# Router logits split into two halves around the last pair of the next batch's input projection (decoder layer, Trainium2)

## The reference

```
x = layernorm(x + mamba(x))          # rmsnorm, in_proj to xi and z (1024 each), causal conv of 4 taps, silu,
                                     # x_proj, softplus(dt), scan over 16 states, y*silu(z), out_proj
x = layernorm(x + depool(x, ctx))    # rmsnorm @ W_in + a decayed sum over context patches + residual
x = layernorm(x + moe(x))            # router: softmax(x @ Wr), 8 experts, top 1, rank in the expert by a
                                     # running count over all tokens, capacity 448, relu MLP 512 -> 2048 -> 512
```

## Time and profile before

| | us |
|---|---|
| median of three runs | 2603.05 |
| the profiled execution, its own time | 2615.71 |
| its span, first to last instruction | 2613.9 |
| PE busy in the span | 2438.4 (93%) |
| DVE busy | 2081.8 (80%) |
| POOL busy | 1786.7 (68%) |
| ACT busy | 1749.5 (67%) |

### The profile page before, as it was taken

The page is one execution under the profiler, slowest core; times in us unless marked ns, Lnnn a source line. Parts: engine busy times, 40 slices in busy tenths (PEclk is TensorE's granted clock), DMA queues, the critical chain, the costliest instruction groups (busy, mean ns, idle before and its releaser), DMA issues.

```text
span 2613.9 us, 33259 instructions
## 1 busy us (share of the span) xinstructions
PE 2438.4 (93%) x11291; PEld 2070.1 (79%) x11291; DVE 2081.8 (80%) x2288; ACT 1749.5 (67%) x4011; POOL 1786.7 (68%) x1045
## 2 busy tenths in 40 slices
PE   7698999999999999999999999997879999999997
PEld 6686787878788787878878787785658989989896
DVE  4899999999999999999999999998833445444452
ACT  5677888888888888888888888887633333333331
POOL 1989999999999999999999999999600101001100
PEclk9899999999999999999999999998979999999998
DMA  6041202212020221202122020211233333234320
GB/s 205 15 132 67 85 15 85 71 36 89 13 91 15 85 75 33 89 18 85 33 75 79 22 92 15 78 50 50 85 127 120 125 125 125 100 128 139 132 75 18
DMA packets 90901, 202.62 MB, mean 78 GB/s; under 512 B 7997, under 2 KB 16843, under 8 KB 90751
## 3 DMA queue, kind: packets, MB, share of 16 engines
q1 hardware_dynamic: 81534, 179.21, 21.1%
q0 software_dynamic: 5120, 14.21, 1.7%
q10 hardware_dynamic: 4096, 7.34, 0.9%
HBM read 171.32 MB, written 29.95 MB: 77 GB/s over the span
## 4 chain that ended last, share of the span: by engine, by line
PE 54%; POOL 25%; DVE 8%; issue 5%; ACT 4%; DMA 3%; SPq 0%; POOLq 0%; DVEq 0%; ACTq 0%
POOL arena L1003 14%; PE work L1683 12%; PE y L1664 11%; PE ring L1683 11%; PE work L1442 7%; PE work L1471 5%; DVE ring L1313 4%; POOL arena L1008 4%; POOL arena L1014 3%; DMA arena<-bc_rows 2%; PE work L1486 2%; ACT ring L858 1%; POOL arena L936 1%; POOL arena L934 1%; POOL arena L932 1%
## 5 line engine op out<-in xcount | busy, mean ns | idle before, releaser
L1003 POOL TENSOR_TENSOR arena<-arena 128x896 f32<-128x896 f32 x512 | 1056.7, 2090 | 20.6 <-PE y L1664 10.1
L858 ACT ACTIVATE ring<-arena,small 128x224 f32<-128x224 f32 x2048 | 794.4, 436 | 138.3 <-DVE arena L1322 106.1
L1313 DVE TENSOR_TENSOR_SCAN ring<-ring,arena 128x896 f32<-128x896 f32 x400 | 809.4, 2024 | 59.3 <-POOL arena L1003 33.5
L1664 PE MATMUL y<-arena,cst_sb 128*128 128x224 f32 x3584 | 775.5, 369 | 75.7 <-POOL arena L1014 57.8
L1664 PEld LDWEIGHTS y<-arena,cst_sb 128*128 128x128 f32 x3584 | 699.5, 199 | 147.4 <-POOL arena L1014 64.1
L1027 POOL DMA_INDIRECT out<-res,ids x32 | 48.9, 1529 | 639.4 <-DVE mst L1368 540.2
L1322 DVE TENSOR_TENSOR arena<-ring,arena 128x896 f32<-128x896 f32 x400 | 433.3, 1083 | 6.0
L1442 PE MATMUL work<-arena 128*128 128x224 f32 x2000 | 428.1, 372 | 6.7 <-DVE arena L1093 6.2
L1442 PEld LDWEIGHTS work<-arena 128*128 128x128 f32 x2000 | 400.9, 203 | 19.1 <-issue 6.8
L1383 DVE SCALAR_TENSOR_TENSOR hidden_lo<-work,hidden_hi 128x448 fp32r<-128x448 f32 x128 | 79.9, 625 | 349.7 <-ACT hidden_hi L902 349.7
L902 ACT ACTIVATE hidden_hi<-work 128x448 fp32r<-128x448 f32 x128 | 69.8, 546 | 374.0 <-PE work L1683 374.0
(11 more groups left out here) (211 smaller groups left out, 3300.3 us busy)
## 6 DMA issues: line engine op xcount, KB each, us to landing
weights<-in_w SPq DMA_DIRECT2D x64, 1024.0 KB, 7.3
arena<-bc_rows SPq DMA_DIRECT2D x128, 448.0 KB, 4.4
arena<-in_ctx SPq DMA_DIRECT2D x16, 896.0 KB, 5.6
expert_rows<-x2e SPq DMA_DIRECT2D x1, 7224.0 KB, 30.1
arena<-in_xT SPq DMA_DIRECT2D x16, 448.0 KB, 6.5
arena<-in_x SPq DMA_DIRECT2D x16, 448.0 KB, 3.7
out<-arena ACTq DMA_DIRECT2D x32, 224.0 KB, 2.3
xrow<-expert_rows SPq DMA_DIRECT2D x7, 903.0 KB, 11.8
```

What stands on the lines that cost most here:

```text
L858: last = nc.scalar.activation(decays[s % 2][:, i * L:(i + 1) * L], delta[:, k, :], ACT.Exp, scale=a_neg[:, n:n + 1])
L1003: nc.gpsimd.tensor_tensor(u[:, u_of(b, s)], dx[:, k:k + 1, :].to_broadcast([P, QN, L]), bc[:, 0, q * QN:(q + 1) * QN, :], ALU.mult).then_i ...
L1313: nc.vector.tensor_tensor_scan(states, h, u_flat[:, u_of(b, s), :], 0.0, ALU.mult, ALU.add).then_inc(scan_done, 1)
L1664: last = nc.tensor.matmul(o, ident, u[:, u_of(b, s), i, :], start=False, stop=(q == Q - 1 and i == QN - 1), skip_group_check=True)
```

## The change

`PE_AT` puts `xi3.0` ahead of the logits, the first half of the logits (`rt.0`) between `xi3.0` and `xi3.1`, and the second half (`rt`) behind `xi3.1`. `routing` on PE gains the place `rt.0` in the steps that have `xi3`; the last batch's step and the drain keep what they had. `FIRST_PART`, which sorts the pieces of a bank, now looks for a part `.0` first; the order in every bank stays as it was.

```diff
         PE_AT = {"xi0.0": 0, "xi0.1": 0.01, "xi1.0": 0.02, "xi1.1": 1, "xi2.0": 1.01, "xi2.1": 1.02, "tx0": 4, "tx1": 4.01,
-                 "rt": 4.02, "xi3.0": 4.03, "xi3.1": 4.04, "out0.0": 6, "out0.1": 7, "out0.2": 7.01, "out0.3": 7.02,
+                 "xi3.0": 4.02, "rt.0": 4.03, "xi3.1": 4.04, "rt": 4.05, "out0.0": 6, "out0.1": 7, "out0.2": 7.01, "out0.3": 7.02,
...
-        FIRST_PART = lambda at, job: at[job if job in at else job + ".0"]
+        FIRST_PART = lambda at, job: at[job + ".0" if job + ".0" in at else job]
...
-                    if b == NB:
+                    if b != LAST and b != NB + 1:
                         yield "rt.0"
                         logits(b, (0,))
                     yield "rt"
-                    logits(b, (1,) if b >= NB else (0, 1))
+                    logits(b, (0, 1) if b == LAST else (1,))
```

## The result

The changed kernel takes 2635.17 us (median of 4 runs, 2626.92 to 2645.29), the kernel before 2603.59 (4 runs). The ratio is 1.0134, 95% interval 1.0111 to 1.0157: slower by 31.6 us, where +14 was forecast (2617 us, range 2594 to 2628). The profiled execution took 2645.29 us with a span of 2643.5, so 29.6 us more than the profiled one before. Both profiled executions are slower than the medians, by 10 and 12 us, so their difference may be read as that of the medians, to some 2 us.

What follows compares the result with a forecast made beforehand. PE, DVE and POOL bound a step in turn. Thirteen steps go from 1477.1 to 11 x 115.11 + 2 x 112.58 = 1491.4 us, +14.3 on the median 2603.05: about 2617 us, range 2594 to 2628.

Steps and rivals of the forecast that it cites:

- the two kinds of steps: Steps before: PE pauses for POOL 28 us after y (mean 112.58 us), or arrives there without a pause (114.37 us).
- The pause of 0.63 us: PE's wait for ACT's copy ahead of the logits; goes, worth 8.2 us at most, taken at nothing.
- The stretch worked out from rows of before: PE from xi3.0 to y, step at 995: done 0.85 us earlier, pause for POOL grows from 1.94 to 2.8 us.
- The falls during xi3 go: Clock falls at the logits or xi3, 9 of 13 steps before, go; they were cheap.
- a fall on y comes in most steps: 3.6 us of quiet ahead of y lowers the clock there; 11 of 13 steps taken.
- The price of such a step: Length of a step whose clock falls on y: 115.11 us, 2.53 us more than one with PE early.
- 312 and 1107: The two steps before whose clock fell on y itself: 115.14 and 115.08 us; 11 steps expected like them.
- The fall behind dt1: Clock fall after the 2.16 us pause ahead of dt1; before, in 7 of 7 late steps, 2 of 5 others.
- the late steps: Steps where PE reaches the next wait for POOL without a pause; seven before, mean 114.37 us.
- that rival: Clock holds ahead of y and every step has PE early: -13.6 us, 2589 us; chance 0.22.
- the second rival: Falls on y replace falls in xi3, as many late steps as before: 2603 us, give or take 3; chance 0.12.
- The third rival: DVE (L1164) waits for the later logits, with the clock as before: +3.9 us, 2607 us; chance 0.06.

Runs made afterwards that it cites:

- mid: Changed kernel with both halves of the logits between xi3.0 and xi3.1; 2607.52 us, ratio 1.0020 to the kernel before.
- fillb3: Changed kernel with the four matmuls of xi3.1 made three times more behind the last logits; 2622.80 us, ratio 1.0083 to the kernel before.
- bdup: Kernel before with the second half of the logits made again behind xi3, their semaphore raised only then; 2628.77 us, ratio 1.0101.
- fillb: Changed kernel with the four matmuls of xi3.1 made once more behind the last logits; 2607.13 us, ratio 1.0026 to the kernel before.
- fill1: Changed kernel with the four matmuls of xi3.1 made once more ahead of the last logits; 2625.45 us, ratio 1.0100 to the kernel before.
- behind: Changed kernel with all of xi3 first, then both halves of the logits; 2641.74 us, ratio 1.0158 to the kernel before.
- fill3: Changed kernel with xi3.1 made four times, ahead of the last logits; 2645.30 us, ratio 1.0165 to the kernel before.
- bfill1: Kernel before with the four matmuls of xi3.1 made twice; 2619.87 us, ratio 1.0067.

## Why the prediction was right and wrong

**What bounds the kernel, and the two kinds of steps**: right. PE alone is not the bound, an early PE only waits for POOL. The pause of 0.63 us gone was worth nothing, as costed, and `mid` shows it without the loss beside it.

**The stretch worked out from rows of before**: right to 0.3 us. Pause ahead of y 2.8 us forecast, 2.50 measured at 1245.04, since POOL was 0.4 us earlier than at 995 (2.72 on average of the 13 steps); logits ready 6.3 us after tx0 forecast, 6.2 measured.

**The falls during xi3 go, a fall on y comes in most steps**: right. 12 of 13 instead of the 11 I took, and none at xi3.

**The price of such a step**: this is the term that failed. "I take 11 of the 13 steps as like 312 and 1107", at 115.11 us. Those were steps whose clock fell some 0.3 us after y had begun, with 16 matmuls in 4.98 us (4.8 from start to start). With 3.4 us of quiet instead of 1.9 the fall comes ahead of y, and y runs wholly at the low clock, 6.06 us. Ten of the twelve steps took 116.18 us on average, 1.07 more than I took, or 10.7 us; the share of slow steps (11 of 12 against 10.2) adds 2.1, and the other two steps (115.60 and 111.76 us) take 0.3 off. Together these are the 12.5 us that the twelve steps lack (forecast 12/13 of 1491.4, or 1376.7; measured 1389.15). The thirteenth step, which I had counted like the others (+1.1), came out 3.35 us longer (106.60 and 109.95 us from tx0 to tx0). I had the bound at hand: 16 matmuls that xi3 made slowly at 769 took 5.9 us, and with it y would have been 2.8 us late, not 1.7. It belonged in the range at least.

**The fall behind dt1**: I let it come in through the mean of the late steps. It is 0.77 of the 2.15 us a step. The steps of before had both a long and a short form of it; in the changed kernel ten steps in a row or nearly repeat at 116.0 to 116.6 us, each with the long one. It goes with PE's coming late and not with the slow y as such: `fillb3` has it without any fall on y. Why the steps settle at this length was not tested.

**The rivals**: the clock did not hold; pauses of 2.39 to 2.71 us behind four small matmuls were enough in eight steps. The rule of the Trainium skill that spoke for that rival ("TensorE: Matmul & The Clock Gate", "Why this matters for your kernels") warns of longer idle stretches than these. In the second rival, "each harmless alone" is the prediction's own reading; the page of the Trainium skill that it names does not say it. The third rival did not happen (L1164 waited in no step), but its price was far too low (`bdup` lost 27 us by it), and that it did not happen is luck: the logits were ready within 0.04 us of DVE's reading. So taking nothing for this term was right in size and not by its reasoning, which counted on DVE's slack.

## What to carry to other kernels

Where PE waits for another engine inside an otherwise dense program, look at what lies directly ahead of the wait: a block of small matmuls there acted as more waiting did (y wholly slow behind small matmuls and 2.5 us in the changed kernel, and behind big ones and 3.75 us in one step of `mid`), and the big matmuls behind it pay at half the clock. Put the small ones between big ones, and leave something big as the last piece before a wait. And where a sum rests on a mean of a few odd steps, ask what the same effect costs when it is not cut short.

## What was not expected of the hardware

Filling a pause with useless matmuls made a kernel faster: 20 us of extra work over 13 steps took 1.1% off the time (`fillb` against the changed kernel). Kernels that differ only in such details also scatter very differently from run to run: `fill1` by 25 us and the changed kernel by 18 us over four runs, `behind` by 7 and `fill3` by 3, the kernel before by 10 over 19 runs. `bfill1` reached over 34 us in ten runs. What decides it was not found. A part lies outside the change: from the last turn of `tx0` to the end, where all these kernels do the same work, the profiled executions took between 726 and 737 us.
